# A causal attention stage: the mask moved from TensorE into VectorE's row-minimum pass, and q's rotation shared between three engines

## The reference

```python
h = take(weight, x)                               # 8 x 512 x 256
q, k, v = (einsum('btm,mhd->bthd', layernorm(h), w) for w in (w_aq, w_ak, w_av))
q, k = rope(q), rope(k)     # halves: even*cos - odd*sin, even*sin + odd*cos
s = einsum('bihd,bjhd->bhij', q, k) / 128
s = s - 1e30 * (i < j)                            # causal mask
p = softmax(s)
h = h + einsum('bhij,bjhd->bihd', p, v) @ w_o
h = h + ffn(layernorm(h))                         # router, top-k, 8 experts
```

## Time and profile before

| | before |
|---|---|
| median of the runs | 1285.78 us (1285.78 to 1285.96) |
| profiled execution, its own time | 1286.61 us |
| its span, first to last instruction | 1284.8 us |
| granted TensorE clock, mean | 0.957 |
| TensorE busy | 1148.5 us, 89% |
| VectorE busy | 912.1 us, 71% |
| GpSimd busy | 740.8 us, 58% |
| ScalarE busy | 609.5 us, 47% |

### The profile page before, as it was taken

The page is one execution under the profiler, slowest core; times in us unless marked ns, Lnnn a source line. Parts: engine busy times, 40 slices in busy tenths (PEclk is TensorE's granted clock), DMA queues, the critical chain, the costliest instruction groups (busy, mean ns, idle before and its releaser), DMA issues. The chain is left out here.

```text
span 1284.8 us, 21944 instructions
## 1 busy us (share of the span) xinstructions
PE 1148.5 (89%) x7255; PEld 985.3 (77%) x7255; DVE 912.1 (71%) x1980; ACT 609.5 (47%) x1306; POOL 740.8 (58%) x783
## 2 busy tenths in 40 slices
PE   3899999999999999999999978015999999999995
PEld 2688888878878878878888863004999999999994
DVE  5888888898888998988988853775555555553522
ACT  4455545545555445545555543102654654655541
POOL 3776676776766776766766730005654744744425
PEclk9999999999999999999999998556999999999998
DMA  5000100100100100100100001304423623624212
GB/s 184 5 14 1 38 30 0 37 29 0 41 24 0 41 24 9 43 13 33 33 1 34 17 2 34 106 0 133 116 34 99 133 34 99 132 34 99 34 17 33
DMA packets 42170, 57.60 MB, mean 45 GB/s; under 512 B 8896, under 2 KB 34944, under 8 KB 41984
## 3 DMA queue, kind: packets, MB, share of 16 engines
q0 software_dynamic: 13824, 21.24, 9.2%
q1 hardware_dynamic: 28288, 35.58, 8.3%
HBM read 35.71 MB, written 16.91 MB: 41 GB/s over the span
## 5 line engine op out<-in xcount | busy, mean ns | idle before, releaser
L1125 DVE TENSOR_TENSOR hT_lo<-hid,hT_hi 128x512 fp32r<-128x512 f32 x128 | 89.4, 699 | 178.8 <-ACT hT_hi L1243 178.8
L268 ACT ACTIVATE prob<-bank,row_min 128x512 f32<-128x512 f32 (+3 forms) x256 | 136.1, 532 | 113.1 <-DVE row_min L389 113.0
L199 POOL TENSOR_SCALAR prob<-prob,row_inv 128x512 f32<-128x512 f32 (+3 forms) x256 | 135.0, 540 | 68.2 <-DVE row_inv L393 66.7
L1241 ACT ACTIVATE hid<-up,b_e 128x512 f32<-128x512 f32 x128 | 88.1, 688 | 154.8 <-PE up L1308 143.6
L339 DVE TENSOR_TENSOR pT_lo<-bank,pT_hi 128x384 fp32r<-128x384 f32 (+1 forms) x192 | 114.2, 595 | 50.8 <-ACT pT_hi L248 50.6
L949 POOL DMA_INDIRECT got<-routed_rows,tokens x64 | 85.8, 1341 | 102.7 <-DVE tokens L1119 85.4
L212 POOL TENSOR_TENSOR kT_lo<-k_cos,kT_hi 128x512 fp32r<-128x512 f32 x64 | 84.2, 1315 | 78.1 <-ACT kT_hi L248 78.1
L248 ACT ACTIVATE oT_hi<-bank 128x512 fp32r<-128x512 f32 x64 | 38.4, 599 | 186.5 <-PE bank L519 178.5
L206 POOL TENSOR_TENSOR q_cos<-q_cos,q_sin 128x512 f32<-128x512 f32 x64 | 82.3, 1287 | 55.1 <-DVE q_sin L376 55.0
L969 POOL DMA_INDIRECT out<-y,tokens x64 | 103.2, 1613 | 17.3 <-issue 14.8
L389 DVE TENSOR_REDUCE row_min<-bank 128x1 f32<-128x512 f32 (+3 forms) x256 | 112.4, 480 | 0.2
(11 more groups left out here) (196 smaller groups left out, 3855.8 us busy)
## 6 DMA issues: line engine op xcount, KB each, us to landing
raw<-in_w SPq DMA_DIRECT2D x16, 1024.0 KB, 8.1
emb_res<-emb SPq DMA_DIRECT2D x8, 512.0 KB, 3.7
out<-h SPq DMA_DIRECT2D x8, 512.0 KB, 2.9
routed_rows<-x SPq DMA_DIRECT2D x8, 512.0 KB
x<-in_wq SPq DMA_DIRECT2D x1, 1024.0 KB, 5.3
x<-in_wk SPq DMA_DIRECT2D x1, 1024.0 KB, 5.0
x<-in_wv SPq DMA_DIRECT2D x1, 1024.0 KB, 7.2
x<-in_wo SPq DMA_DIRECT2D x1, 1024.0 KB, 10.0
```

What stands on the lines that cost most here:

```text
L199: nc.gpsimd.tensor_scalar(pr, pr, row_inv[:, h % 2, k:k + 1], 1.0, ALU.mult, ALU.mult).then_inc(s["norm_done"], 1)
L268: nc.scalar.activation(prob[:, h % 2, col:col + w], s_ps[bk][:, pc:pc + w], ACT.Exp, bias=row_min[:, h % 2, k:k + 1], scale=-1.0, accum_ou ...
L1125: nc.vector.tensor_tensor(out, in_, hi.bitcast(F32), ALU.subtract)\
L1241: nc.scalar.activation(hid[:, t % 2, :], up_ps[t % 2][:], ACT.Gelu, bias=bias)
```

## The change

Five things are changed.

- **Mask.** The four mask products of a head and their bf16 operands go. `minimum` becomes one instruction that adds a mask row to the scores, scales by -1/128, writes the result to `prob` in SBUF and gives the row's minimum. The mask row is 384 zeros and the 128 x 128 mask; its last w columns serve a block w wide. The exponential works in place in `prob`.
- **Waits.** Since the scores leave their bank with the minimum, TensorE waits for `s_min` where it waited for `exp_done`. `minimum` now waits for the transposes of the head two before (`t_done`), which the exponential did.
- **q's rotation.** VectorE makes only q·cos. ScalarE copies q's halves, swapped, from PSUM to `q_sin`; GpSimd multiplies them by sin, and adds. TensorE waits for `q_swap` where it waited for `q_rope`. k is rotated as before, and one table serves both.
- **Order.** In a slot, GpSimd adds k before it takes q's low part; ScalarE starts with the swap and takes the first high part of the transposes before that of q.
- **Loop and setup.** The hardware loop over batches 1 to 6 is written out. ScalarE prepares one mask tile instead of three tiles, and takes the high part of w_o in slot 0 of the first batch.

```diff
-            with eng.Fori(1, B - 1) as b:
+            for b in range(1, B - 1):
...
+            nc.gpsimd.memset(mask_row[:, 0:T - P], 0.0).then_inc(s["mask_ready"], 1)
...
+                if x == "q":
+                    cos, sin = q_cos, q_sin
+                    after(pool, "q_swap", n + 1)
+                    nc.gpsimd.tensor_tensor(sin[:], sin[:], rope_t[:, 1, :], ALU.mult)\
+                        .then_inc(s["q_sin"], 1)
+                    after(pool, "q_sin", n + 1)
...
+                        add(b, h, "k")
                         low(b, h, "q")
-                        add(b, h, "k")
...
-                after(act, "t_done", 3 * (n - 2) + 3)
-                nc.scalar.activation(prob[:, h % 2, col:col + w], s_ps[bk][:, pc:pc + w], ACT.Exp,
+                pr = prob[:, h % 2, col:col + w]
+                nc.scalar.activation(pr, pr, ACT.Exp,
                                      bias=row_min[:, h % 2, k:k + 1], scale=-1.0,
...
+            def swap(b, h):
+                n = b * H + h
+                after(act, "q_mul", n + 1)
+                after(act, "q_add", n)
+                nc.scalar.activation(q_sin[0:64, :], proj_ps[0][64:128, :], ACT.Copy)
+                nc.scalar.activation(q_sin[64:128, :], proj_ps[0][0:64, :], ACT.Copy)\
+                    .then_inc(s["q_swap"], 1)
...
+                    if ok(h - 2):
+                        t_high(b, h - 2, 0)
                     if live:
                         qk_high(b, h, "q")
-                    if ok(h - 2):
-                        t_high(b, h - 2, 0)
...
+            def rope_q(b, h):
+                n = b * H + h
+                after(dve, "q_proj", n + 1)
+                after(dve, "q_lo", n)
+                nc.vector.tensor_tensor(q_cos[:], proj_ps[0][:], rope_t[:, 0, :], ALU.mult)\
+                    .then_inc(s["q_mul"], 1)
...
-                nc.vector.tensor_reduce(row_min[:, h % 2, k:k + 1], s_ps[bk][:, pc:pc + (ib + 1) * P],
-                                        AX.X, ALU.min).then_inc(s["s_min"], 1)
+                nc.vector.tensor_tensor_reduce(prob[:, h % 2, col:col + w], s_ps[bk][:, pc:pc + w],
+                                               mask_row[:, T - w:T], scale=-1.0 / D, scalar=3e38,
+                                               op0=ALU.add, op1=ALU.min,
+                                               accum_out=row_min[:, h % 2, k:k + 1])\
+                    .then_inc(s["s_min"], 1)
...
-                    after(pe, "k_rope" if kt else "q_rope", b * H)
+                    after(pe, "k_rope" if kt else "q_swap", b * H)
...
-                    last = nc.tensor.matmul(s_ps[bk][:, pc + ib * P:pc + w], ident_bf[:], mask_bf[:],
-                                            start=False, stop=True)
...
-                        after(pe, "exp_done", TB * (n - 1) + 1)
+                        after(pe, "s_min", TB * (n - 1) + 1)
                         scores(b, h - 1, [3])
```

More of the change, by code:

```diff
@@ L52, in build_attention @@
         w_o = [sb(f"wo_{p}", [P, H, M], F32R) for p in ("hi", "lo")]
[L54 to L57, removed]
+        rope_t = sb("rope_t", [P, 2, T])
+        mask_row = sb("mask_row", [P, T], BF16)
         neg_half = sb("neg_half", [P, TB])
@@ L86, in build_attention @@
         o_ps, t_ps = bank[4], [bank[5], bank[4], bank[5]]
-        names = """wq_in wk_in wv_in wo_in tables_in w_hi w_lo consts
+        names = """wq_in wk_in wv_in wo_in tables_in mask_ready w_hi w_lo consts
             ids_in emb_in res_in stats_done aggr_done var_eps rstd_done xn_ready xt_tr xt_hi xt_lo
-            q_proj k_proj v_proj q_rope k_rope q_add k_add q_hi k_hi q_lo k_lo v_hi v_lo
+            q_proj k_proj v_proj q_mul q_swap q_sin k_rope q_add k_add q_hi k_hi q_lo k_lo v_hi v_lo
             s_done s_min exp_done inv_done norm_done t_done t_hi t_lo o_done o_hi o_lo
@@ L203, in add @@
                 n = b * H + h
-                cos, sin = (q_cos, q_sin) if x == "q" else (k_cos, k_sin)
-                after(pool, f"{x}_rope", n + 1)
+                if x == "q":
[4 more added lines that the diff above has]
+                    after(pool, "q_sin", n + 1)
+                else:
+                    cos, sin = k_cos, k_sin
+                    after(pool, "k_rope", n + 1)
                 nc.gpsimd.tensor_tensor(cos[:], cos[:], sin[:], ALU.add).then_inc(s[f"{x}_add"], 1)
@@ L250, in _ @@
             act.wait_ge(s["tables_in"], 48)
[L251 to L254, removed]
+            nc.scalar.activation(mask_row[:, T - P:T], mask_f, ACT.Copy, scale=-float(D))\
+                .then_inc(s["mask_ready"], 1)
             def xt(b):
@@ L306, in body @@
                     live = ok(h) and h < H
+                    if live:
+                        swap(b, h)
                     if ok(h - 3):
@@ L323, in body @@
                         qk_high(b, h, "k")
+                    if isinstance(b, int) and b == 0 and h == 0:
+                        act.wait_ge(s["wo_in"], 16)
+                        hi_of(w_o[0][:], wraw_o, "w_hi")
                     if ok(h - 1):
@@ L560, in scores @@
                     w = (ib + 1) * P
-                    products(s_ps[bk][:, pc:pc + w],
-                             [([q[:, h % 2, ib * P:(ib + 1) * P] for q in qT],
-                               [x[:, h % 2, 0:w] for x in kT])], stop=False)
-                    last = nc.tensor.matmul(s_ps[bk][:, pc + ib * P:pc + w], ident_bf[:], mask_bf[:],
-                                            start=False, stop=True)
+                    last = products(s_ps[bk][:, pc:pc + w],
+                                    [([q[:, h % 2, ib * P:(ib + 1) * P] for q in qT],
+                                      [x[:, h % 2, 0:w] for x in kT])])
                 last.then_inc(s["s_done"], 1)
```

43 lines of the change are left out of this document (21 added, 22 removed).

## The result

The changed kernel takes 1267.9 us (median of four runs, 1267.0 to 1270.0) against 1285.9: ratio 0.986, interval 0.985 to 0.988. That is faster, as forecast, and at the slow edge of the range (1246 to 1268). The profiled execution took 1270.0 with a span of 1268.2; the one of before had 1284.8, so the two traces differ by 16.6. TensorE's wait in front of the router's first transpose marks the end of attention in both: 768.5 before, 747.0 after. So attention gave 21.5 us, and what follows it took 4.9 more (521.2 against 516.3). Most of the 4.9 lies in the router's search loop: one turn of it, its *period*, takes 3.29 us where it took 3.04.

A forecast was written before the change was run, and what follows sets the result against it. TensorE's list bounds most slots, VectorE's lateness the batch's end. Masks 23.6, slot 6 4.4, slot 7 3.5, edges 0.5: 32.0 us off 1286.6 gives 1254.6, as median 1253.8; range 1246 to 1268, own range 1247 to 1259.

The forecast's parts named there:

- (a): Slots 6 and 7: only the masks gain, since another wait there was as late; 1266 or 1262 us; chance 0.13.
- (c): TensorE's score products: a mask's price is its own pitch, 0.19 us a slot, 12 us less gain, 1266; chance 0.05.
- (b): Slots with gathers: GpSimd becomes the bound; 1264 us at 0.5 us each, 1274 at 1 us; chance 0.08.
- Masks, 0.38 a slot: TensorE: without four mask matmuls a head, a middle slot goes from 10.94 to 10.56 us; 62 slots give 23.6 us.
- VectorE's pass: VectorE's row minimum with the mask added runs at the reduction's rate, about 0.69 us; net 1.0 us a slot less.
- Rival (d): VectorE: the new row-minimum pass runs at the scan's rate, 1.9 us more a head; 1276 us; chance 0.05.
- ScalarE: right in sum: ScalarE: two swap copies (1.1 us) and exponentials from SBUF (0.08) raise a middle slot from 5.85 to 7.1 us, hidden.
- GpSimd's pass "at nothing": GpSimd: the extra pass of 1.29 us a slot fills idle holes and costs nothing, with a margin of 0.8 us.
- Rival (e): VectorE's new pass and GpSimd shut each other out; slower, 1300 us, at most 1323; chance 0.06.
- Slot 6: Batch's end: VectorE's work fits, 11.67 goes to 10.56 us, 0.73 beyond the masks, in six batches 4.4 us.
- Slot 7: Batch's end: k_sin's wait shrinks, xT_lo's grows; 0.97 us saved, 0.38 of it masks; 0.59 x 6 = 3.5 us.
- Later stages shift as they are: Behind attention: the later stages keep their length and only start earlier.

The follow-up runs named there:

- odd-width kernel: The changed kernel with each x2 normalisation on VectorE cut into two pieces, of 129 and 127 columns: 1276.9 us, ratio 0.9924.
- e9_both: e6_act with two of the four normalisations of the next batch's embeddings (slot 7) also made by ScalarE: 1257.1 us, ratio 0.9768.
- padded kernel: The changed kernel with 28 one-column memsets on VectorE ahead of the router's search loop: 1264.1 us, ratio 0.9833.
- e6_act: The changed kernel with a batch's four x2 normalisations moved from VectorE to ScalarE, the shift -mean/std made by GpSimd: 1260.4 us, ratio 0.9801.

## Why the forecast was right in sign and 14 us too good

By the traces, 10.5 us are missing in attention and 4.9 behind it, of 32.0. The forecast's own range, 1247 to 1259, was missed. That the time lies inside the wide one, by 0.1 us, is luck: it reached to 1268 for rivals (a), (c) and part of (b), and the missing time has mostly other causes.

**Masks, 0.38 a slot: right.** 10.94 to 10.56, with TensorE never idle in such a slot. Reading pitches instead of lengths gave the number, and rival (c) is out. What the text lacked is the condition: the mask part alone brought 5.2 us of attention time, since the chain over v_lo was right behind.

**VectorE's pass: right.** 681 and 286 ns, 83 ns for the accumulator. VectorE is busy for 7.56 us in a middle slot, where 8.87 less 1.0 would be 7.87. The difference is the 0.34 for the accumulator: its four reads stand in the trace as rows of their own, but the next pass starts at the same moment (both at 224.68), so they cost next to nothing. Rival (d) is out.

**ScalarE: right in sum** (7.26 against 7.1). The swap copies follow each other at 0.61 us, not 0.50: that pitch was of another pair of copies. In slot 7, where q's chain sets the end, the 0.1 us counts. An exponential of 512 columns takes 716 ns from SBUF and took 689 from PSUM: 27 ns, near the 20 of the rows.

**GpSimd's pass "at nothing": the step that failed.** Its own time is right: 1.29 us, 8.48 busy in the middle slot, kT_lo ending at 10.8. The prediction counted who reads GpSimd's results and gave them a margin. It didn't count who else needs GpSimd's pauses. The second of x2's two normalisations ran in the pause ahead of k_lo, which the change filled ("both holes are filled"). Slot 5 comes to 11.44 instead of 10.56 in batches 1 to 6, and to 11.39 in the last: 0.88 x 6 + 0.83 = 6.1 us. Rival (e) had the right resource and the wrong side: GpSimd lost next to nothing (its pass at such an opening takes 1.35 us for 1.29), VectorE stood still, and not in the new pass but in the instruction whose 0.68 against 0.41 was in the earlier trace rows. The prediction called that "somewhat longer" and gave it no price. Its sign for rival (b), TensorE waiting for prob, came too, in slot 7: 0.65 us in each batch. xT_lo still comes later there and ends the slot, so this wait hasn't set its length.

The Trainium skill (SBUF — State Buffer, SBUF: two separate sides) says that between GpSimd and an instruction of VectorE that uses two ports or reads two SBUF inputs, whichever starts first gets the shared pair of ports for the whole instruction and the other fully blocks. On VectorE's side the traces agree: an opening each at 260.2 and 261.5 in the odd-width kernel, 2.80 us for two instructions of 0.41, 2.43 for three. That GpSimd blocks in its turn no run here shows beyond the 0.06 us above.

**Slot 6, 0.25 a batch short (1.5 us).** This is the same term again. GpSimd issues a gather there, the extra pass starts right behind it (265.98) and q's sum behind that, so the sum is done 8.2 us into the slot, in a middle slot 6.4; q_hi, the first exponential and v_hi stand in a row on ScalarE, and v_lo ends as the next slot starts:

```profile
268.70 0.64 ACT L254 ACTIVATE qT_hi<-q_cos 128x512 fp32r<-128x512 f32 x1 [2.22 <-POOL q_cos L212]
...
269.24 0.70 ACT L272 ACTIVATE prob<-prob,row_min 128x512 f32<-128x512 f32 x1
...
269.94 0.58 ACT L254 ACTIVATE v_hi<-bank 128x512 fp32r<-128x512 f32 x1
...
270.55 0.69 DVE L354 TENSOR_TENSOR v_lo<-bank,v_hi 128x512 fp32r<-128x512 f32 x1 [1.30 <-ACT v_hi L254]
```

The prediction summed VectorE's work and found that it fits; a busy sum says nothing of a chain that starts late. This cause is read from the trace; no experiment undid it alone.

**Slot 7: the mechanism right, the size off.** The k_sin wait went and the chain over q_hi and xT_lo ends the slot, with 2.65 us from the first exponential to the next slot. The forecast put that exponential at 9.8 us of the slot and it came at 10.2, because q_cos came 0.33 later and the swap copies took 0.1 longer: 0.44 x 6 = 2.6 us. e9_both bears the chain out by moving q_cos. The prediction left q_cos where it was ("I leave it there"), but it waits for 1/std, which GpSimd starts 1.67 us into the slot instead of 1.34, behind the pass that the change added.

**The rest.** The three shortfalls make 10.2 us. Up to the start of batch 1 the change gave 0.5 us (106.10 to 105.62), where six slots at 0.38 and the edges' 0.5 make 2.8: another 2.3 short. Slot 1 of the first batch is 8.72 us before and varies from 9.0 to 10.3 in the kernels with the rotation part and the new pass, most of which don't differ there; why, no run shows. Against that 2.0 us came back, half of it in slot 7 of batches 1 and 6, which took 13.93 before and not the 13.41 of the earlier trace rows. Together these are the 10.5.

**"Later stages shift as they are": failed by 3.6 us.** Fourteen periods of the search took 46.1 us instead of 42.5. It goes with how many instructions lie ahead of the loop, as the padded kernel shows. In the prediction's words the unrolled loop was "Nothing"; alone it is, but the mask part, with the loop written out, has the slower search and the rotation part, without, has not. The last 1.3 us are TensorE's wait for the load of b_rows, 3.3 before and 4.6 in this execution. That wait is 4.5 in the kernel with only the loop written out and 3.4 in e6_act, so it varies by itself and says nothing of the change.

**What the whole hung on.** The forecast took the order of GpSimd's instructions for a filling of holes and never priced its reverse. The new order is worth 54 us: with the extra pass GpSimd has no time left in a batch's later slots for the waits that the old order brings.

## What to carry over

When an edit fills an engine's pauses, list not only who waits for that engine but who works in its pauses: an operation that is slower beside it than alone names itself in the groups. Parts of a change don't add: price each with the others undone, and if only one binds at a time, expect little from it alone. After a change of code size, compare the period of every tight loop behind it before explaining the end time. Count every batch, too: a term that is read from one middle batch can come seven times, and the first batch can behave otherwise.

## What the hardware showed that was not expected

- A TENSOR_SCALAR from SBUF to SBUF on VectorE, beside GpSimd passes without a pause, gets in once per GpSimd instruction: 0.41 us becomes up to 1.49, and four of 0.33 take 4.16 together. ScalarE does two of the same 128x256 blocks in 1.09 (595 ns for one), beside GpSimd too.
- The custom sum-and-minimum pass over PSUM with a bf16 row from SBUF runs at the plain reduction's rate (681 ns at 512 columns) and is not blocked: none of its 256 instructions takes more than 692 ns, beside GpSimd passes or not.
- A loop of VectorE instructions ran at 3.04 or 3.29 us a turn (mean of fourteen), with the same instructions, by how many others lay ahead of it.
